# Eight-head attention: the last block's 53 destinations stand twice on the partitions, two heads to a unit

## The reference, cut to what matters

```python
Wh = (x @ W.T).reshape(N, H, C)                    # N = 3125, H = 8, C = 32
e = e_left[src] + e_right[dst]                     # one number for each edge and head
e = where(e >= 0, e, 0.2 * e)
e_exp = exp(e - segment_max(e, dst)[dst])
alpha = e_exp / (segment_sum(e_exp, dst)[dst] + EPS)
out = segment_sum(Wh[src] * alpha[:, :, None], dst)  # back to N x 256
```

## Time and profile before

| | us |
|---|---|
| median of 3 runs (lowest, highest) | 3741.9 (3736.48, 3748.98) |
| the profiled execution: its own time | 3744.81 |
| its span, from the first to the last instruction | 3743.1 |
| TensorE busy in it | 3425.8 (92%) |
| VectorE busy | 2828.5 (76%) |
| ScalarE busy | 2523.6 (67%) |
| GpSimd busy | 300.4 (8%) |
| mean TensorE clock granted, of full speed | 0.972 |

### The profile page before, as it was taken

One profiled execution on the slowest core, in us unless ns is written; L12 is line 12 of the kernel. 1 busy time (PEld: TensorE's weight loads), 2 busy tenths in 40 slices (PEclk: granted clock), 3 DMA queues, 4 the chain that ended last, 5 costly groups with the idle time before them and its releaser, 6 DMA issues. The chain is left out here.

```text
span 3743.1 us, 70138 instructions
## 1 busy us (share of the span) xinstructions
PE 3425.8 (92%) x27405; PEld 2680.2 (72%) x27406; DVE 2828.5 (76%) x4285; ACT 2523.6 (67%) x4088; POOL 300.4 (8%) x279
## 2 busy tenths in 40 slices
PE   6999889989999898998668999699999999999999
PEld 4565566666666666666458999588878888788777
DVE  7999999999999999999662222665556555676594
ACT  5899899999999999999710111366656665676532
POOL 1000010000000000000003444000000000000000
PEclk9999999999999999999859999899999999999999
DMA  5433211112114121111268885323323232423101
GB/s 163 155 109 140 99 55 65 64 55 73 55 63 202 55 73 55 62 67 55 66 202 267 238 237 150 128 104 106 113 76 119 106 114 75 173 104 121 38 22 35
DMA packets 146630, 398.54 MB, mean 106 GB/s; under 512 B 20163, under 2 KB 92252, under 8 KB 128252
## 3 DMA queue, kind: packets, MB, share of 16 engines
q1 hardware_dynamic: 127542, 354.64, 26.8%
q0 software_dynamic: 15552, 36.16, 4.1%
q10 hardware_dynamic: 3206, 3.20, 0.3%
HBM read 331.96 MB, written 61.99 MB: 105 GB/s over the span
## 5 line engine op out<-in xcount | busy, mean ns | idle before, releaser
L994 PE MATMUL hd_psT<-ident,hd_scores 128*128 128x128 f32 (+1 forms) x5000 | 721.6, 282 | 13.6 <-ACT hd_scores L896 13.6
L905 ACT ACTIVATE hd_probsT<-hd_psT 128x768 f32<-128x768 f32 (+1 forms) x800 | 658.9, 850 | 69.0 <-PE hd_psT L994 69.0
L959 DVE SCALAR_TENSOR_TENSOR hd_scores<-el_heads,hx 128x3136 f32<-128x3136 f32 x200 | 694.9, 3475 | 0.0
L1008 PE MATMUL hd_psO<-hd_probsT,hx 128*32 128x128 f32 (+1 forms) x10000 | 571.3, 281 | 135.1 <-ACT hd_probsT L905 135.1
L963 DVE CUSTOM_DVE_ANT_0 hd_scores<-hd_scores,mask_heads 128x3136 f32<-128x3136 f32 x200 | 684.1, 3421 | 8.6
L896 ACT ACTIVATE hd_scores<-hd_scores,hd_negmax 128x1664 f32<-128x1664 f32 (+1 forms) x400 | 647.9, 1620 | 18.8 <-DVE hd_negmax L963 18.8
L994 PEld LDWEIGHTS hd_psT<-ident,hd_scores 128*128 128x128 f32 (+1 forms) x5000 | 531.8, 140 | 162.7 <-issue 162.7
L1526 PE MATMUL ly_psO<-hx_a,ly_probsT 128*128 128x256 f32 x2500 | 584.0, 381 | 0.0
L1008 PEld LDWEIGHTS hd_psO<-hd_probsT,hx 128*32 128x32 f32 (+1 forms) x10000 | 316.9, 108 | 332.3 <-ACT hd_probsT L905 225.7
L1475 ACT ACTIVATE ly_probsT<-ly_psT 128x768 f32<-128x768 f32 (+1 forms) x300 | 248.4, 828 | 391.8 <-PE ly_psT L1515 391.6
L1526 PEld LDWEIGHTS ly_psO<-hx_a,ly_probsT 128*128 128x128 f32 x2500 | 453.9, 189 | 71.4 <-issue 16.6
(11 more groups left out here) (337 smaller groups left out, 3957.3 us busy)
## 6 DMA issues: line engine op xcount, KB each, us to landing
ly_mask<-mask_dram SPq DMA_DIRECT2D x75, 1568.0 KB, 6.6
mask_heads<-mask_dram SPq DMA_DIRECT2D x48, 1568.0 KB, 6.6
moe_w<-in_L_ffn_w SPq DMA_DIRECT2D x144, 512.0 KB
mask_dram<-logc SPq DMA_DIRECT2D x200, 196.0 KB, 1.9
el_heads<-el_dram POOLq DMA_DIRECT2D x4, 1568.0 KB, 19.3
el_heads<-el_slope_dram POOLq DMA_DIRECT2D x4, 1568.0 KB, 23.0
el_heads<-el_dram SPq DMA_DIRECT2D x4, 1568.0 KB, 10.1
el_heads<-el_slope_dram SPq DMA_DIRECT2D x4, 1568.0 KB, 14.2
```

The source lines that it names most:

```text
L905: nc.scalar.activation(pT[:, gi % 2, 0:w], psT[gi % 2][:, 0:w], ACT.Copy).then_inc(s_ev, 1)
L959: nc.vector.scalar_tensor_tensor(sc[:, c, :], el[:, h, 0, :], hx[:, b, o:o + 1], el[:, h, 1, :], ALU.subtract, ALU.min).then_inc(s_lk, 1)
L994: last = nc.tensor.transpose(psT[gi % 2][0:r, t * P:(t + 1) * P], sc[:, u % 3, c0:c0 + r], g["ident"][:, :])
L1008: last = nc.tensor.matmul(psO[B % 3][cg * CH:(cg + 1) * CH, h * P:(h + 1) * P], hx[0:r, tt, c0:c0 + CH], pT[0:r, gi % 2, t * P:(t + 1) * P ...
```

## The change

The last block of each pass is *packed*. Its 53 destinations, rounded up to 64 (`HALFP`), stand on partitions 0 to 63 for one head and again on 64 to 127 for the next, so that a unit covers two heads and the block takes two units (`PAIRS`) in place of four. `UPB` is the number of units of each block, `FIRST` the first unit of each block, `UNIT` the block and place of each unit; the waits that counted multiples of HG count by them. There are 98 units a pass, 196 in all.

For a packed block the mask's 64 rows are loaded twice, to either half; the left terms are loaded pair by pair, each row to 64 partitions (`load_el_pair`, four DMAs of half the size in place of two); the right terms of the pairs are copied at the start of the phase into a small tile `er` by eight DMAs of 64 numbers. The left terms of the next pass are now issued in the loop's turn of block 24, ahead of the turn of block 25 in which its mask is issued, and `place` moves heads to other buffers. `products` makes two matmuls of 64 columns for each tile. The store is two DMAs. In `node_phase` the last part of y is loaded as four full blocks and 64 rows, and the last block of y is cleared first.

```diff
 NPART = NB // PART
...
 assert NPART * PART == NB and EXTRA > 0
+HALFP = P // 2
+PAIRS = HG // 2
+assert EXTRA <= HALFP
@@ -680,11 +683,13 @@
...
                     if full < PART:
-                        sp.wait_ge(s_pad, 1)
+                        sp.wait_ge(s_pad, 2 if y_in is not None else 1)
                         sp.dma_start(x[0:EXTRA, FULL, :], x_in[FULL * P:N, :]).then_inc(s_in[p], 16)
                     if y_in is not None:
-                        sp.dma_start(y[:, b:b + PART, :],
-                                     y_in[b * P:(b + PART) * P, :].rearrange("(b p) f -> p b f", p=P)).then_inc(s_yin[p], 16)
+                        sp.dma_start(y[:, b:b + full, :],
+                                     y_in[b * P:(b + full) * P, :].rearrange("(b p) f -> p b f", p=P)).then_inc(s_yin[p], 16)
+                        if full < PART:
+                            sp.dma_start(y[0:HALFP, FULL, :], y_in[FULL * P:FULL * P + HALFP, :]).then_inc(s_yin[p], 16)
                 if x_out is not None:
@@ -705,7 +710,7 @@
...
                     if y_in is not None:
-                        dve.wait_ge(s_yin[p], 16)
+                        dve.wait_ge(s_yin[p], 16 if p < NPART - 1 else 32)
                     if gelu:
@@ -735,6 +740,8 @@
...
             if layernorm:
+                if y_in is not None:
+                    nc.vector.memset(y[:, FULL, :], 0.0).then_inc(s_pad, 1)
                 nc.vector.memset(x[:, FULL, :], 0.0).then_inc(s_pad, 1)
@@ -828,9 +835,18 @@
...
         s_el = [sem(f"s_el{h}") for h in range(HG)]
+        er = sb("right_terms_of_pairs", [P, PASSES * PAIRS])
+        s_er = sem("s_right_terms_of_pairs")
         block = ctx.enter_context(nc.Block())
         BLOCKS = PASSES * NB
-        UNITS = BLOCKS * HG
+        UPB = [HG] * (NB - 1) + [PAIRS]
+        UNITS = PASSES * sum(UPB)
+        FIRST = [sum(UPB) * q + sum(UPB[:b]) for q in range(PASSES) for b in range(NB)] + [UNITS]
+        UNIT = [(B, k) for B in range(BLOCKS) for k in range(UPB[B % NB])]
+        packed = lambda B: B % NB == NB - 1
+        masks_in = lambda B: 16 * (B // 2 + len([L for L in range(2, B + 1) if packed(L) and L % 2 == B % 2]))
+        stored = lambda B: 16 * sum(1 + packed(L) for L in range(B % 3, min(B, BLOCKS), 3))
+        place = lambda q, k: (k + q * PAIRS) % HG
         CG = P // CH
@@ -839,21 +855,44 @@
...
             rows = (g["el_dram"], g["el_slope_dram"])[i]
-            eng.dma_start(el[:, h, i, :], rows[q * HG + h:q * HG + h + 1, 0:NS].broadcast_to([P, NS])).then_inc(s_el[h], 16)
+            eng.dma_start(el[:, place(q, h), i, :], rows[q * HG + h:q * HG + h + 1, 0:NS].broadcast_to([P, NS])).then_inc(s_el[place(q, h)], 16)
+
+        def load_el_pair(eng, q, k, i):
+
+            rows = (g["el_dram"], g["el_slope_dram"])[i]
+            for e in range(2):
+                h = q * HG + 2 * k + e
+                eng.dma_start(el[e * HALFP:(e + 1) * HALFP, place(q, k), i, :],
+                              rows[h:h + 1, 0:NS].broadcast_to([HALFP, NS])).then_inc(s_el[place(q, k)], 16)
...
         def _(sp):
+            for q in range(PASSES):
+                for k in range(PAIRS):
+                    for e in range(2):
+                        h = D + q * HG + 2 * k + e
+                        sp.dma_start(er[e * HALFP:(e + 1) * HALFP, q * PAIRS + k:q * PAIRS + k + 1],
+                                     hx[0:HALFP, NB - 1, h:h + 1]).then_inc(s_er, 16)
             for B in range(2, BLOCKS):
-                sp.wait_ge(s_nm, (B - 1) * HG)
-                b = B % NB
+                sp.wait_ge(s_nm, FIRST[B - 1])
+                q, b = B // NB, B % NB
                 if B == L1_LOOPS // P:
                     sp.wait_ge(s_lout, 16)
-                sp.dma_start(mask[:, B % 2, :], g["mask_dram"][b * P:(b + 1) * P, :]).then_inc(s_mask[B % 2], 16)
-                if b == 0:
+                if packed(B):
+                    for e in range(2):
+                        sp.dma_start(mask[e * HALFP:(e + 1) * HALFP, B % 2, :],
+                                     g["mask_dram"][b * P:b * P + HALFP, :]).then_inc(s_mask[B % 2], 16)
+                    for k in range(PAIRS):
+                        sp.wait_ge(s_lk, FIRST[B - 1] + k + 1)
+                        load_el_pair(sp, q, k, 0)
+                        load_el_pair(sp, q, k, 1)
+                else:
+                    sp.dma_start(mask[:, B % 2, :], g["mask_dram"][b * P:(b + 1) * P, :]).then_inc(s_mask[B % 2], 16)
+                if packed(B) and q + 1 < PASSES:
                     for h in range(HG):
-                        sp.wait_ge(s_lk, (B - 1) * HG + h + 1)
-                        load_el(sp, B // NB, h, 0)
-                        load_el(sp, B // NB, h, 1)
+                        sp.wait_ge(s_lk, FIRST[B - 1] + PAIRS + h + 1)
+                        load_el(sp, q + 1, h, 0)
+                        load_el(sp, q + 1, h, 1)
@@ -864,10 +903,11 @@
...
                 i = B % 3
-                pool.wait_ge(s_ex, (B + 1) * HG * 2)
+                pool.wait_ge(s_ex, FIRST[B + 1] * 2)
                 if B >= 3:
                     pool.wait_ge(s_y, B - 2)
-                nc.gpsimd.tensor_tensor(rden[:, i, :], den[:, i, :, 0], den[:, i, :, 1], ALU.add).then_inc(s_sum, 1)
+                n = UPB[B % NB]
+                nc.gpsimd.tensor_tensor(rden[:, i, 0:n], den[:, i, 0:n, 0], den[:, i, 0:n, 1], ALU.add).then_inc(s_sum, 1)
             halves_added(0)
@@ -881,14 +921,20 @@
...
                 pool.wait_ge(s_y, B + 1)
-                nc.gpsimd.dma_start(y_dram[b * P:(b + 1) * P, q * P:(q + 1) * P], y[:, B % 3, :]).then_inc(s_store[B % 3], 16)
-            for i in range(3):
-                pool.wait_ge(s_store[i], 16 * len(range(i, BLOCKS, 3)))
+                if packed(B):
+                    rows_ = y_dram[b * P:b * P + HALFP, q * P:(q + 1) * P].rearrange("r (k e c) -> r k e c", e=2, c=CH)
+                    for e in range(2):
+                        nc.gpsimd.dma_start(rows_[:, :, e, :], y[e * HALFP:(e + 1) * HALFP, B % 3, 0:PAIRS * CH].rearrange(
+                            "p (k c) -> p k c", c=CH)).then_inc(s_store[B % 3], 16)
+                else:
+                    nc.gpsimd.dma_start(y_dram[b * P:(b + 1) * P, q * P:(q + 1) * P], y[:, B % 3, :]).then_inc(s_store[B % 3], 16)
+            for B in range(BLOCKS, BLOCKS + 3):
+                pool.wait_ge(s_store[B % 3], stored(B))
...
             def exps(u, j):
-                B, k = u // HG, u % HG
+                B, k = UNIT[u]
                 if j == 0:
@@ -905,18 +951,19 @@
...
             def copy_sums(B):
-                act.wait_ge(s_mm, (B + 1) * HG * 4)
+                act.wait_ge(s_mm, FIRST[B + 1] * 4)
                 if B:
                     act.wait_ge(s_yT, B)
-                nc.scalar.activation(oT[:, :, :].rearrange("p h n -> p (h n)"), psO[B % 3][:, 0:HG * P], ACT.Copy).then_inc(s_oT, 1)
+                n = UPB[B % NB]
+                nc.scalar.activation(oT[:, 0:n, :].rearrange("p h n -> p (h n)"), psO[B % 3][:, 0:n * P], ACT.Copy).then_inc(s_oT, 1)
...
                 if B >= 3:
-                    act.wait_ge(s_store[i], 16 * (B // 3))
-                for h in range(HG):
+                    act.wait_ge(s_store[i], stored(B))
+                for h in range(UPB[B % NB]):
                     last = nc.scalar.activation(y[:, i, h * CH:(h + 1) * CH], psY[:, h * CH:(h + 1) * CH], ACT.Copy,
@@ -932,10 +979,10 @@
...
                     copy_out(u, gi)
-                    if gi == 2 and u % HG == 0 and u:
-                        copy_sums(u // HG - 1)
-                    if gi == 2 and u % HG == 1 and u > HG:
-                        rows(u // HG - 1)
+                    if gi == 2 and UNIT[u][1] == 0 and u:
+                        copy_sums(UNIT[u][0] - 1)
+                    if gi == 2 and UNIT[u][1] == 1 and u > HG:
+                        rows(UNIT[u][0] - 1)
                     if gi % 2 == 1 and u + 1 < UNITS:
@@ -947,16 +994,21 @@
...
             def maxima(u):
-                B, h, c = u // HG, u % HG, u % 3
+                (B, h), c = UNIT[u], u % 3
                 q, b = B // NB, B % NB
+                at = place(q, h)
                 if h == 0 and B >= 2:
-                    dve.wait_ge(s_mask[B % 2], 16 * (B // 2))
+                    dve.wait_ge(s_mask[B % 2], masks_in(B))
                 if b == 0 and q:
-                    dve.wait_ge(s_el[h], 32 * q)
+                    dve.wait_ge(s_el[at], 96 if h >= HG - PAIRS else 32)
+                if packed(B):
+                    dve.wait_ge(s_er, 16 * 2 * PASSES * PAIRS)
+                    dve.wait_ge(s_el[at], 96 if q else 64)
                 if u >= 3:
...
                 o = D + q * HG + h
-                nc.vector.scalar_tensor_tensor(sc[:, c, :], el[:, h, 0, :], hx[:, b, o:o + 1], el[:, h, 1, :],
+                right = er[:, q * PAIRS + h:q * PAIRS + h + 1] if packed(B) else hx[:, b, o:o + 1]
```

(25 more changed lines are left out.)

## The result

| us | before | after |
|---|---|---|
| median (lowest, highest) of 6 runs each | 3742.21 (3736.48, 3748.98) | 3766.55 (3763.09, 3768.14) |
| the profiled execution: its own time, its span | 3744.81, 3743.1 | 3768.14, 3766.2 |

The changed kernel is slower by 24.3 us: the ratio is 1.0061, with a 95% interval of 1.0043 to 1.0080. The forecast was 3760.6, and slower; the measured median is some 6 us above it, and just above the upper end of the stated range, 3766.

The account below looks back on a forecast made before the run. VectorE was taken to set the pace, one unit in 6.88 us. Units -27.5, pass 0 stalls +37.3, pass 1 stall +8.4 and phase end +0.5 gave +18.7 us: 3760.6, range 3729 to 3766.

Parts of the forecast that it names:

- the units: Attention phase, VectorE: 200 units become 196, four at 6.88 us each saved in full, -27.5 us.
- the mask is late because of where it stands: End of pass 0: block 25's mask, queued behind the left terms, makes VectorE wait; stalls there counted +37.3 us.
- a half costs a whole: SP's queue: a 64-partition DMA takes 4.0 us like a whole one; stalls 37.3 and 8.4 us; chance 0.51.
- the floor of 3.89: SP's queue: lowest price of one whole DMA, 3.89 us, from 1.606 MB at 413 GB/s.
- the products are covered: TensorE in packed units: products cost the same to twice the time (+2.6 us a unit), hidden by 4.7 us of slack.
- the clock is no bound inside the phase: TensorE's clock drops while it waits for the mask, but this costs nothing inside the attention phase.
- the end: Uncovered end of the attention phase: shorter turning back and scaling, longer products and second store; -1.2 to +1.6, taken +0.5 us.
- the total: Whole kernel: -27.5 + 37.3 + 8.4 + 0.5 = +18.7 us, forecast 3760.6.
- only bytes count: SP's queue: half DMAs cost half; stall 17.3 us at mask 25, none in pass 1; -9.7, 3732.2; chance 0.30.
- halves overlap in part: SP's queue: two halves cost 1.5 DMAs; stall 27.3 us, none in pass 1; +0.3, 3742.2; chance 0.12.
- TensorE becomes the bound: Packed units: products at three times the cost, pass 1 ends 4.1 us later; 3764.7 with full price; chance 0.03.
- no stall: At (25, 0): mask 25 lands before 1133, or the change doesn't do what it says; -27, 3715; chance 0.04.

Follow-up runs that it names:

- The kernel with whole loads and the mask ahead: Changed kernel with each pair of half DMAs made one 128-partition DMA (second head left out) and block 25's mask before the last two heads' left terms: 3722.2, ratio 0.9946.
- the interleaved one: Changed kernel with two heads alternating on partitions (2r + e), one DMA per pair, and block 25's mask ahead of pass 1's second head's left terms: 3720.4, ratio 0.9938.
- the interleaved kernel: Changed kernel with two heads alternating on partitions (2r + e), one 128-partition DMA per mask or pair, order of issues kept: 3739.7, ratio 0.9992.
- with whole loads: Changed kernel, order kept, each pair of half DMAs made one DMA to 128 partitions (second head left out in the last block): 3738.3, ratio 0.9997.
- the three edits made alone: Each alone in the kernel before: next stage's edits 3744.2 (1.0018); last block's store as two DMAs 3740.9 (1.0003); eight small right-term DMAs with a wait 3740.2 (0.9981).

## Why the prediction was right, step by step, and where it was short

**Right: the units.** 196 steps at L1011 and L1015 with the durations of before, and -27.5 in VectorE's own line: +14.1 = -27.5 + 41.5. The kernel with whole loads and the mask ahead has -25.2 with 1.93 of stall left, the interleaved one -26.6 with none.

**Right: the mask is late because of where it stands.** Its wait is the one predicted, at (25, 0), released by the DMA of a mask. Moving it alone gave back 15.4 us.

**Right in kind, slightly high in size: a half costs a whole.** 206 GB/s were predicted where halves flow, and 217 measured. From the issue of the first half at about 1095.2 to the start of (25, 0) at 1171.3, less the fixed 2.7, there are 73.4 us for 19 DMAs: 3.86 each where I took 4.0. The two parts give the same: ten halves up to the step of (24, 1) at 1136.5, less the 2.7, are 38.6 us, 3.86 each, and the nine whole DMAs from there to 1171.3 are 34.8 us, 3.87 each. So the two stalls of pass 0 were 6.89 + 27.87 = 34.8, predicted 37.3, and that at (49, 1) 6.73, predicted 8.4. The price from the ten DMAs of before (4.08) was too high, since their start was thin; the floor of 3.89, from 413 GB/s, was the better end. At long transfers the rule of the Trainium skill, "SBUF — State Buffer", "Door 1: The DMA port swizzle", that 64 partitions get half of the full rate, agrees: 217 against 425. By its figures at 1 MiB ten halves would count as an estimated 8.4 wholes; this queue, which never empties, does not show that, with 3.86 us for a half and 3.87 for a whole.

**Right: the products are covered.** The timeline of TensorE, with the products of the packed unit (24, 0), while VectorE is at (24, 1):

```profile
1136.74 0.66 PE L1063 MATMUL hd_psO<-hd_probsT,hx 128*32 128x64 f32 x24
1137.33 0.91 PE L1047 MATMUL hd_psT<-ident,hd_scores 128*128 128x128 f32 x4
```

24 instructions of 64 columns take 0.59 us to the next transposes, where 12 of 128 columns took 0.56. The lower bound, the same time, holds to 0.03 us a group; the slack of 4.7 us was not needed. Every second column costs no more: in the interleaved kernel it is 0.61.

**Right: the clock is no bound inside the phase.** While TensorE had nothing to do its granted clock fell, to 0.52 in a stretch of 3 us, close to the level of 1.2 GHz, and in the stretch from 1187, with work again, it was 1.00, 2.4 GHz:

```profile
1142.00:1145.00 3.00, 0.00 (x0) 0.00 (x0) 1.43 (x2) 1.53 (x1) 0.00 (x0) 0.52 0.99 414
...
1187.00:1190.00 3.00, 2.48 (x35) 1.75 (x33) 2.96 (x3) 3.00 (x6) 0.00 (x0) 1.00 0.00 0
```

VectorE had no idle time in between: the two units by which it is ahead covered the catching up.

**Short by a little: the end.** Predicted +0.5, measured +1.6, the upper end of its bounds. The rows behind it:

```profile
1856.50 1.76 PE L1047 MATMUL hd_psT<-ident,hd_scores 128*128 128x128 f32 x7
...
1858.19 1.29 PE L1063 MATMUL hd_psO<-hd_probsT,hx 128*32 128x64 f32 x24
...
1859.41 1.08 PE L1071 MATMUL hd_psY<-hd_fold,hd_sumsT 128*128 128x32 f32 x8
...
1864.90 0.97 PE L1063 MATMUL hd_psO<-hd_probsT,hx 128*32 128x64 f32 x24 [0.32 <-ACT hd_probsT L951]
...
1866.35 0.63 PE L1071 MATMUL hd_psY<-hd_fold,hd_sumsT 128*128 128x32 f32 x4 [0.47 <-ACT hd_sumsT L958]
1867.02 0.46 ACT L967 ACTIVATE hd_y_stage<-hd_psY,hd_rden 128x32 f32<-128x32 f32 x2 [0.72 <-PE hd_psY L1071]
1867.78 1.24 POOL L927 DMA_DIRECT2D y_dram<-hd_y_stage  x2 [2.77 <-ACT hd_y_stage L967]
```

From the last VectorE step to the end of the last products it is 2.2 us longer (10.85 before, 13.01 now); folding, turning back and scaling are about 1.0 shorter (0.63 and 0.46 against 1.08 and 0.82); the second store adds 0.5. The prediction had two things wrong in the first of these, which it bounded by the price of the products alone.

One is a displaced piece of work. The row at 1859.41 turns back the sums of block 48, the block before. That is done behind the first unit of block 49; with four units in the block three more followed, and now only the last one does, so it stands in the uncovered end. It is there in the kernels that have no stall at this place too: with whole loads the same stretch takes 11.5 us, 0.7 more than before.

The other is the clock. The stall of 6.73 us just ahead of the last unit ran TensorE dry, and the last unit's transposes began at the low clock: seven of them take 1.76 us, against 0.98 in the earlier trace rows, and the products behind them 1.29, against 0.97 with whole loads. With these the stretch is 1.5 us longer than in the kernels without a stall. I had named the clock for the middle of the phase, where it is covered, and not for its end, where nothing is. In the kernel with only the mask moved the stall is the same, 6.83, but the stretch takes 15.6 us, 4.1 more than without a stall (its tail is 25.6 us, 1834.3 to 1859.9, against 23.0), and TensorE's six us after the stall ran wholly at the lower level. The stretch in that kernel, and the one in the changed kernel:

```profile
1837.00:1843.00 6.00, 6.00 (x64) 5.16 (x65) 0.17 (x1) 3.50 (x5) 0.18 (x1) 0.50 0.01 3
```

```profile
1855.00:1861.00 6.00, 5.51 (x69) 4.76 (x69) 0.17 (x1) 4.04 (x6) 0.18 (x1) 0.68 0.01 3
```

0.50 and 0.68. So here a stall ahead of an uncovered end is worth its own length and 1.5 to 4.1 us more, and those differ from kernel to kernel. In the next stage nothing came later behind the first sum of y: to its last it is 20.56 us, before and after. The 0.9 us ahead of the first sum are not its extra clear and DMA: made alone, these leave that time at 7.6, as before, and in the kernels with the whole change it is anything from 7.6 to 8.8. What makes it vary is not known.

**Mis-sized: the total.** By the trace the sum should have been +16.6 us in place of +18.7: the price of a slot was too high by 4.2 us over both ends of the passes, and 1.1 at the end and 0.9 ahead of the next sum were missing, so that it came nearer than its terms did. The median says +24.3. The rest, some 8 us, lies outside the phase, in work that the change does not touch, and the prediction put that at nothing. This, and not the highest price of a slot for which the range was drawn, is what took the median to its upper end. The traces of both kernels run again place it: of 26.7 us between them (3764.15 and 3737.45), 16.6 are in the phase and 10.0 in the loop over the experts. The row of the page for the experts' hidden values, of before run again and of the changed kernel run again (the idle time is what grows):

```profile
L1972 ACT ACTIVATE moe_hidden<-moe_ps_h 128x512 f32<-128x512 f32 x64 | 38.2, 597 | 326.8 <-PE moe_ps_h L1937 326.8
```

```profile
L2028 ACT ACTIVATE moe_hidden<-moe_ps_h 128x512 f32<-128x512 f32 x64 | 38.2, 597 | 336.8 <-PE moe_ps_h L1993 248.2
```

The loop takes 363.6 to 377.0 us in all nine traces of the changed kernel and its variants, and 354.1 to 356.4 in four of the five traces of before and of before with one edit; the fifth, the first trace of before, has 362.8. So it is not the same in every execution of one kernel; and the 377.0 belong to an execution of 3751.8 us of the interleaved kernel, whose median is 3739.7. Medians against phases say the same: every variant of the change lies 7 to 11 us above its phase (+24.3 against +16.6; with the mask moved +14.4 against +3.4; interleaved with the mask ahead -20.0 against -26.6). None of the three edits made alone lengthens the loop. **This stays open**: it was not tried with the rest of the change alone (the packed block's arithmetic without its loads), and whether the cause is in the data's place, in the code's or in how the loop happens to start is not known.

The rivals: *only bytes count* and *halves overlap in part* fall with 217 GB/s and 226 on two queues; *TensorE becomes the bound* falls with 0.59 us for the products; *no stall* with 27.87.

## What to carry to other kernels

Before moving a DMA in a full queue, write down what stands ahead of it, in slots: here a slot is 3.86 us, whether the DMA reaches 128 partitions or 64, and two bounds for one unknown, halves at half price or at full, gave forecasts 28 us apart. When two things share the partitions, interleave them (2r + e) so that one DMA reaches all 128, and issue what is wanted first ahead of what is wanted later; here that turned +24 us into -20. A stall just ahead of the end of a phase is paid twice, in the wait and in TensorE's clock behind it. And when units are taken out of the last block, look at what was hidden behind them: here the folding of the block before came to stand in the open.

## What the runs showed that was not expected

Halves on two queues together move 226 GB/s with the DMA engines shown busy for all of the time, the same as on one queue. An access pattern in which neighbouring partitions take turns between two rows (64 by 2 by columns) flows at 411 GB/s, like a plain load:

```profile
1098.00:1116.00 18.00, 16.06 (x208) 11.57 (x208) 17.87 (x14) 16.69 (x25) 1.22 (x2) 1.00 0.99 411
```

And a stage that comes after the changed one, and shares nothing with it but the chip, took from 354 to 356 us in four traces and from 363 to 368 in nine (377 in one more), without anything in it having been changed. By the traces and the medians that stands behind most of the 8 us that the phase doesn't explain; its cause is open.
